# Splitting the layer-norm normalisation of stage 1 between VectorE and GpSimd in an eight-core transformer layer

## The reference

```python
x = x + _layernorm(_L0_attn_ref(_layernorm(x), Wq, Wk, Wv, Wo))
x = x + _layernorm(_L0_ffn_ref(_layernorm(x), gate_w, up_w, down_w, gate_s, up_s, down_s))

def _layernorm(x, axis=-1, eps=1e-5):
    m = jnp.mean(x, axis=axis, keepdims=True)
    v = jnp.var(x, axis=axis, keepdims=True)
    return (x - m) / jnp.sqrt(v + eps)
```

## Time and profile before

| | us |
|---|---|
| median of 2 runs | 4184.69 (4176.9 to 4192.48) |
| the profiled execution, its own time | 4186.81 |
| its span, slowest core (6) | 4185.2 |
| spans of the eight cores | 4152.2 to 4185.2 |
| mean granted TensorE clock of the cores | 0.874 to 0.877 |

### The profile page before, as it was taken

How to read it: one execution, slowest core, us unless ns; L and a number is a source line. 1 busy time by engine, 2 the same in 40 slices (tenths; PEclk the granted TensorE clock), 3 DMA queues, 4 the chain that set the end, 5 groups by cost and what they waited for, 6 DMA issues and landing times.

```text
span 4185.2 us, 34406 instructions; the slowest of 8 cores (4152.2 to 4185.2 us)
## 1 busy us (share of the span) xinstructions
PE 3139.7 (75%) x12480; PEld 1163.9 (28%) x12480; DVE 1372.3 (33%) x1252; ACT 712.3 (17%) x718; POOL 357.6 (9%) x284
## 2 busy tenths in 40 slices
PE   5652678988888946788887777824888888878881
PEld 1110234433343412111111112301333333333330
DVE  3675614645545537222222221063000000000006
ACT  2221000000000000444444443211000000000000
POOL 0000000000000000323323331000000000000000
PEclk9775889999999978888888888957999999989995
DMA  5664921011111171111111102322333333243333
GB/s 160 200 181 104 144 64 60 36 58 55 56 60 55 40 126 46 45 41 41 41 41 41 41 11 71 51 80 71 61 61 59 62 61 61 51 96 56 56 56 120
DMA packets 183204, 294.30 MB, mean 70 GB/s; under 512 B 6656, under 2 KB 121344, under 8 KB 180864
## 3 DMA queue, kind: packets, MB, share of 16 engines
q0 software_dynamic: 44352, 102.77, 15.1%
q1 hardware_dynamic: 138688, 189.34, 14.4%
HBM read 323.54 MB, written 71.30 MB: 94 GB/s over the span
## 4 chain that ended last, share of the span: by engine, by line
PE 66%; DVE 13%; DMA 9%; ACT 5%; issue 3%; another core or an unknown queue 2%; POOL 2%; ACTq 0%; DVEq 0%; SPq 0%; POOLq 0%
PE psA L159 24%; PE psB L159 20%; PE psD L159 8%; PE psC L159 7%; PE psE L159 6%; DMA xa<-xctx 3%; ACT esb L547 2%; DMA lns<-ln_scr 2%; POOL esb L557 2%; DVE hdn L748 1%; DVE lno L273 1%; DVE lno L271 1%; ACT gt L745 1%; DVE esb L557 1%
## 5 line engine op out<-in xcount | busy, mean ns | idle before, releaser
L159 PE MATMUL psA<-h,gsb 128*128 128x512 bf16 x1408 | 335.3, 400 | 157.8 <-DVE hdn L748 127.8
L159 PE MATMUL psA<-lns,wk_sb 128*128 128x512 bf16 x1024 | 244.5, 400 | 145.2 <-DMA lns<-ln_scr 78.9
L557 POOL TENSOR_TENSOR esb<-esb,mask_sb 128x1024 bf16<-128x1024 bf16 x128 | 271.2, 2118 | 811.6 <-ACT esb L547 811.6
L159 PE MATMUL psB<-h,usb 128*128 128x512 bf16 x1408 | 311.1, 379 | 0.0
L748 DVE SCALAR_TENSOR_TENSOR hdn<-psB,us_sb,gt 128x1024 bf16<-128x1024 f32 x44 | 56.5, 1283 | 724.3 <-ACT gt L745 724.3
L557 DVE TENSOR_TENSOR esb<-esb,mask_sb 128x1024 bf16<-128x1024 bf16 x128 | 106.2, 830 | 572.4 <-ACT esb L547 572.4
L159 PE MATMUL psC<-wv_sb,lns 128*128 128x512 bf16 x1024 | 236.5, 385 | 16.5 <-DMA wv_sb<-wv 16.5
L159 PE MATMUL psD<-esb,vsb 128*128 128x512 bf16 x512 | 161.1, 397 | 113.1 <-POOL esb L557 79.7
L159 PE MATMUL psD<-wv_sb,lns 128*128 128x512 bf16 x1024 | 235.8, 384 | 13.0 <-DMA wv_sb<-wv 13.0
L159 PE MATMUL psE<-esb,ones_c 128*1 128x512 bf16 x768 | 243.6, 400 | 0.0
L159 PEld LDWEIGHTS psA<-h,gsb 128*128 128x128 bf16 x1408 | 140.5, 102 | 353.8 <-issue 212.1
(11 more groups left out here) (157 smaller groups left out, 3110.5 us busy)
## 6 DMA issues: line engine op xcount, KB each, us to landing
xa<-xctx SPq DMA_DIRECT2D x8, 4096.0 KB, 25.2
gsb<-wg POOLq DMA_DIRECT2D x44, 512.0 KB, 5.2
usb<-wu POOLq DMA_DIRECT2D x44, 512.0 KB, 7.1
dsb<-wd POOLq DMA_DIRECT2D x32, 704.0 KB, 6.3
ln_scr<-lno SPq DMA_DIRECT2D x10, 2048.0 KB, 11.1
lns<-ln_scr SPq DMA_DIRECT2D x8, 2048.0 KB, 10.0
k_scr<-kout SPq DMA_DIRECT2D x128, 128.0 KB, 1.9
v_scr<-vout SPq DMA_DIRECT2D x32, 512.0 KB, 2.7
```

The source lines that it names most:

```text
L159: en.matmul(o, l, r, start=a, stop=z))
L557: en.tensor_mul(b[:], b[:], m)))
```

## The change

The two whole-tile operations of `finish` are cut along the 16 chunks of the model dimension: VectorE does chunks 0 to 10, GpSimd chunks 11 to 15, each with the same two operations on its part. `norm[j]` becomes a list of two points, one for each engine, and everyone who waited for `norm` waits for both. Both engines wait for ScalarE's copies and for the store of the chunk before. Nothing else is touched.

```diff
                 if j >= 1:
-                    p.wt("s", *norm[j - 1])
+                    for sm_, ct_ in norm[j - 1]:
+                        p.wt("s", sm_, ct_)
                 p.dat("s", lambda en: en.copy(rbc[:], psC[:]))
                 cp_tgt[j] = p.dat("s", lambda en: en.copy(bbc[:], psD[:]))
-                eng = "v"
-                p.wt(eng, sS, cp_tgt[j])
                 srcb = xa[j % 4]
-                if j >= 1:
-                    p.wtd(eng, store_done[j - 1])
-                p.dat(eng, lambda en, s_=srcb: en.tensor_tensor(
-                    lno[0][:], s_[:], bcast_ap(rbc, DC, 512), ALU.mult))
-                norm[j] = (p.dsem[eng], p.dat(eng, lambda en: en.tensor_tensor(
-                    lno[0][:], lno[0][:], bcast_ap(bbc, DC, 512), ALU.add)))
-                p.wt("y", *norm[j])
+                tg = []
+                for eng, lo, hi in (("v", 0, 11), ("g", 11, 16)):
+                    p.wt(eng, sS, cp_tgt[j])
+                    if j >= 1:
+                        p.wtd(eng, store_done[j - 1])
+                    n_ = hi - lo
+                    p.dat(eng, lambda en, s_=srcb, l=lo, n=n_: en.tensor_tensor(
+                        lno[0][:, l:l + n, :], s_[:, l:l + n, :], bcast_ap(rbc, n, 512), ALU.mult))
+                    tg.append((p.dsem[eng], p.dat(eng, lambda en, l=lo, n=n_: en.tensor_tensor(
+                        lno[0][:, l:l + n, :], lno[0][:, l:l + n, :], bcast_ap(bbc, n, 512), ALU.add))))
+                norm[j] = tg
+                for sm_, ct_ in tg:
+                    p.wt("y", sm_, ct_)
                 store_done[j] = p.dma("y", "lno0", lambda en, j_=j: en.dma_start(
                     out=ln_scr[:, :, j_ * 512:(j_ + 1) * 512], in_=lno[0][:]))
...
             for i in range(10):
                 if i >= 4:
-                    p.wt("y", *norm[i - 4])
+                    for sm_, ct_ in norm[i - 4]:
+                        p.wt("y", sm_, ct_)
```

## The result

| | before | changed |
|---|---|---|
| profiled execution, its own time, us | 4186.81 | 4212.69 |
| span of the slowest core, us | 4185.2 | 4211.1 |
| undisturbed executions, us | 4176.9 to 4192.5 | 4207.2 to 4219.6 |
| ratio to before | | 1.0072 (95% interval 1.0059 to 1.0084) |

The change makes the kernel 0.72% slower, about 30 us, and the interval is far from 1. (In some executions of every kernel here the cores of one die, or of both, show a lower granted clock and the time is 1 to 12% longer; the ratios, and the times called undisturbed, leave those out.) The forecast was 4215 us, with a range of 4178 to 4240.

A forecast was written before the change was run, and what follows sets the result against it. Stage 1 was taken as bound by a chain of waits with six normalisations, each 4.9 us longer: 6 x 4.9 = +29.4, less 0.7, plus 0.5, +29 us on 4186.8 or the median, said as 4215 us, range 4178 to 4240.

The forecast's parts named there:

- The chain and its factor of six: Stage 1: six normalisations stand on the chain of waits, so x us in one normalisation is worth 6x us of span.
- VectorE's share: Each of VectorE's two operations per chunk in stage 1 shrinks from 8.69 us to 6.03 us.
- GpSimd's share: GpSimd's two operations of 2560 elements per chunk take 5.3 us each, 5.15 or 10.6/7.9 as ends.
- rival 3: GpSimd's time goes by f32 bytes, with exclusion: normalisation 30.4 us, +77 us, 4264 at the far end; chance 0.08.
- Turns in both directions: A chunk's four operations exclude each other whoever comes first: normalisation 22.4 to 22.5 us instead of 17.50.
- rival 1: The engines run side by side in the normalisation: 12.2 us, -32 us, 4155; chance 0.12.
- rival 2: VectorE waits for GpSimd, GpSimd never for VectorE: -5 us, 4182, or about 4186 with GpSimd first; chance 0.12.
- Who is first, and what L244 does: VectorE should win the first turn, either order sums alike; the statistics' L244 waits for GpSimd, so only 0.7 us is gained.
- The sum: Whole kernel: 6 x 4.9 = +29.4 us, less 0.7 at chunk 8, plus 0.5 for waits: +29, 4215 us.
- the sentence that 2% is about what a measurement of this kernel can tell from no change: Whole kernel: 2% is 84 us; chances faster by over 2% 0.01, within 2% 0.96, slower by over 2% 0.03.
- the cost, the wait and the path: Stage 1: operations of 6.03 and 5.3 us, the engines taking turns, and 4.9 us going whole into the chain's loads.

The follow-up runs named there:

- PSUM operands: The changed kernel with VectorE's two operations reading the broadcast rows from psC and psD in PSUM, not rbc and bbc; ratio to before 0.992, undisturbed 4144 to 4149 us.
- the kernel with forced order: The changed kernel with GpSimd's two operations made to wait for VectorE's second, so nothing overlaps; ratio to before 1.0075, undisturbed 4206 to 4216 us.
- the earlier loads: The kernel before with each load issued one turn of the loop earlier, ahead of the store wait in front of it; ratio 0.9958.

## Why the prediction was right, and where it was not

**The chain and its factor of six.** Right. The page's chain has the six normalisations on it, the period grew from 67.3 to 71.2 us, and the experiments scale with it: 0.29% for two rows, 0.72% for five. In stage 1 the median core's last store came 26 us later, 3 less than the sum, and the two profiled executions are 25.9 us apart; the period grew by 4.5 us on average (71.6 against 67.1, four periods from chunk 0 to chunk 8) and not 4.9: the normalisation by 4.8, while load and sums came out 0.3 shorter (25.4 and 19.3 on average against 25.5 and 19.5). Between chunks 8 and 9 it was 3.9.

**VectorE's share, 6.03 us.** Measured 6.02 to 6.03 when it is first in the line.

**GpSimd's share, 5.3 us each.** Measured where nothing was beside it: 5.57 to 5.64 for the first and 5.05 to 5.08 for the second (PSUM operands, and the last chunk of the kernel with forced order). The sum, 10.7, was taken at 10.6. In the line, released by VectorE, the first ended 5.46 us after VectorE's and the second 4.91, where the sum had 5.30 and 5.2 to 5.3. The bytes read hardly matter, and rival 3 falls: two f32 operands are 2.19 ns an element, two bf16 were 2.07 in the earlier trace rows, one of each 1.98. The Trainium skill ("GPSIMD Engine Reference", section 3.1, Elementwise) has an f32 `tensor_tensor` of 2048 elements at 4497 ns, which makes 2.2 ns an element; the trace agrees for the f32 operation (2.19), and the mixed one is faster than that.

**Turns in both directions.** This was the guess that carried the sign, since the trace before showed only VectorE waiting. It held: GpSimd's first takes 11.43 us behind VectorE's and 5.57 ahead of it, and PSUM operands undo both. The Trainium skill ("SBUF — State Buffer", section "Who interferes with whom") has the same rule, and three parts of it are seen here: full exclusion for the whole operation (11.43 us for 5.57), decided by who begins (chunk 0 against chunk 2), and none where VectorE has one SBUF input (6.02 us). That a GpSimd operation that only writes SBUF doesn't contend, which the same section says, no run here shows. Rivals 1 and 2 (side by side; one way only) fall with it.

**Who is first, and what L244 does.** VectorE won the first turn in nine chunks and lost it in chunk 2, where it started 0.4 us after GpSimd; as said, it makes no difference. L244 waited for GpSimd as forecast, in eight of the nine chunks in which one follows the other; in chunk 2 GpSimd was already through.

**The sum.** +29 us were forecast, +30 measured by the ratio (0.72% of 4184, with the interval 25 to 35); the undisturbed executions are at 4207 to 4220 us, the forecast was 4215. That it agrees to 1 us is luck: the chain of the profiled execution grew by 26, and its stage 1 ended at 421 us, not near 426.

**What was wrong: the sentence that 2% is about what a measurement of this kernel can tell from no change.** This is the step that failed; the cost, the wait and the path held. By the forecast's own sum the change was +0.7%, plainly slower and clear of the scatter; by stating its chances only against a bound of 2%, with 0.96 for "within", it put under no difference what its own sum made a loss. The runs showed that far less can be told: the interval of the measured ratio reaches 0.13% (5 us) either way, the eleven undisturbed executions of the changed kernel lie within 12.5 us, and the fastest of them (4207.2) is 15 us above the slowest of the kernel before that ran beside them (4192.5). The scatter that it had before it (4176.9 to 4192.5, 0.4% for two single executions) should have said that a few repetitions resolve 0.3%. With a bound of 0.3% the same cases give slower 0.76 (the forecast and rival 3), no difference 0.12 (rival 2), faster 0.12 (rival 1).

**In the experiments** the miss was the earlier loads: each chunk was 1 us longer than worked out. Some 0.6 of it is TensorE's broadcasts, summed as they run right behind the sums (1.98 us the pair) and measured at half that clock (3.75); 0.3 is the next wait in line, the store of the single `lno` buffer; 0.1 is the statistics, 7.6 us in place of 7.5.

## What to carry to other kernels

Before work is given to GpSimd to relieve VectorE, look where VectorE's operands are: if both are in SBUF and GpSimd reads SBUF too, the two engines take turns and the split costs about GpSimd's time minus VectorE's saving, here 4.8 us a chunk for five rows and 1.8 for two. With one of VectorE's operands in PSUM the same split gains: 12.2 us in place of 17.5. And look for an existing overlap of the two in the trace; VectorE instructions that are lengthened and end a fixed 0.55 us after the other engine's tell that VectorE waits. Whether GpSimd waits too, such rows don't tell; that took a run. And when a wait is taken off a chain, sum the new chain with the waits that come next (here a store) and with TensorE's clock as it is after the idle time that the new chain gives it.

## What the runs showed of the hardware that was not expected

A VectorE operation on one partition of 512 elements (L244, 0.68 us alone) stands in the same line: held up by GpSimd in the 11 to 5 split it took 4.56 to 5.96 us, and it held GpSimd's next by 0.3 us (5.35 against 5.05). How little it moves didn't exempt it.

GpSimd's time goes little by the bytes. Its f32 multiply took 2.34 us for 1024 elements (14 to 2 split) and 5.60 for 2560, which makes (5.60 - 2.34)/1536 = 2.12 ns an element and 0.17 us fixed. If the fixed part is the same elsewhere, one bf16 and one f32 operand (5.06 us for 2560) and two bf16 operands (2.12 for 1024) both come to an estimated 1.91 ns an element. That is 10% under the f32 pair, while the bytes read for an element are 8, 6 and 4.
